# A transformer layer in one Trainium2 program: x's norm in the last four QKV blocks later and behind the evictions, x of two blocks loaded behind a quad of weights

## The chip, the cores and the metric

The program runs on one NeuronCore of one Trainium2 chip. The metric is the device time of one execution in microseconds, lower is better. The kernel before takes 2337.14 us, the median of three runs that lie between 2336.86 and 2337.38. The profile is of one further execution.

## What is computed

One pre-norm transformer layer in float32 on x of shape (2, 2048, 1024): attention with one head of 256, and a feed-forward part with a gate.

```python
def layer(x):
    x = x + attn(layernorm(x))
    return x + ffn(layernorm(x))

def attn(x):                      # D = 256
    q, k, v = split(x @ Wqkv + bqkv, 3)
    return softmax(q @ k.T / 16) @ v @ Wo + bo

def ffn(x):
    s = sum(top_k(x @ gate_w, 2))
    h = relu(x @ up_w) ** 2
    return layernorm(h @ down_w + s * (x @ fc1_w @ expert_w) @ fc2_w) * gamma + beta
```

The change touches only the first part of the program, where the first layernorm and `x @ Wqkv` are computed (QKV).

## The kernel before

**Stages.** The program runs through a short start, QKV (to some 327 us in the trace), attention, and the feed-forward part, which is most of the time. Every product is made of three matmuls: each operand is kept as a high part (rounded to fp32r, made on ScalarE by a copy) and a low part (what the rounding left, subtracted on VectorE), and high*high, high*low and low*high are added in PSUM.

**One list of steps.** `timetable()` writes the order of the whole program as one list of named steps; each engine goes through the list and issues only its own part of each step. In QKV the list is laid out by numbers g = 0 to 95, twelve for each of eight blocks of 512 rows of x (u or t = 0 to 7). In block t, g = 12t to 12t+7 are the halves of the four q and k products (`pe_qk`, lines 958 to 960) and g = 12t+8 to 12t+11 the four v products (`pe_v`, lines 977 to 979). `at(g, ...)` puts a step behind the TensorE work of g; `front(g, ...)` puts it behind the TensorE work of g too, but ahead of all steps that `at` put there. Each engine executes its own queue strictly in this order, the DMAs that it issues included, so a step that waits holds up all that stands behind it on its engine.

**The way of x in blocks 4 to 7.** SP loads x of the block into RAW (`load_x`, line 2186, four DMAs of 512 KB), once block u-2's last turn has been made (`raw_done`). VectorE takes the moments (`x_stats`, line 1552, 16 instructions), GpSimd merges them with a round trip through DRAM (`x_merge`, lines 2065 to 2129) and writes NBX and RX. ScalarE normalizes RAW in place (`x_norm`, line 1211, four instructions for each of j = 0 to 3), VectorE turns it (`x_turn`, line 1558, one for each j), ScalarE and VectorE make the high and low parts (`x_parts`, lines 1172 and 1497, into XA0 or XA1, h and l); every `x_parts` waits for the last turn of its block, as its first line says. The first `pe_qk` of the block waits for the low part.

**The evictions.** `qk_out` (line 1224, ScalarE, tiles OUT and STG) empties one of two PSUM banks. Product i of a block goes into bank i % 2, so `pe_qk` of (t, i) waits for `qk_out` of (t, i-2).

**Quads.** Beside this the kernel forms seven combinations of the four quarters of each feed-forward weight block and writes them to DRAM in high and low parts. One such job (a quad) is: SP loads it (lines 2288 and 2296) into the tiles QR0a or QR1a, VectorE makes sums (`quad_sums`, lines 1671 to 1678), ScalarE the high parts (`quad_high`, 1322 or 1325 and 1172), ScalarE issues their store (1330), VectorE makes the low parts (1686 to 1697), ScalarE issues their store (1337 to 1339, or 1341). Jobs 0 to 9 (u0 to u9) and job 10 (d0) alternate between the two buffers q0 and q1, at g = 4 + 11m/2. The load of a job waits for the stores of the job before it in its buffer. Smaller jobs in the buffers qd and qe (QRd, QRe) follow from g = 68.

**K and V.** From g = 67 SP loads K and V back from DRAM into two small STG buffers (`kv_load`, line 2231), and ScalarE and VectorE split them into KH/KL and VH/VL. KH lies where buffer q0 was, so its first split waits for the store of d0; a load into an STG buffer waits for the split of what was there. At g = 84 and 85 the last V splits and the split of Q stand ahead of `qk_out` of (7, 0). `Q`, `K` and `V` are what attention's first product needs.

```python
    def run(n):
        for step in ahead.pop(n, []) + later.pop(n, []):
...
        def raw_done(u):
            return normed["turn", u, 3] if u > 3 else xt_mm[u, 3]
...
        def x_parts(u, a):
            on.wait_ge(*normed["turn", u, 3])
```

Of the kernel before, what the change touches and what calls it, by code (L numbers as in the profile page):

```python
# [138 lines left out]
def timetable():  # L139
# [6 lines left out]
    def at(n, *step):  # L146
        later.setdefault(n, []).append(step)

    def front(n, *step):
        ahead.setdefault(n, []).append(step)  # L150
# [123 lines left out]
            at(n, "xt_hi", u, a)  # L274
            front(n + 1, "xt_lo", u, a)
    for u in range(4, 8):
        load, moments, norm = {4: (22, 28, 40), 5: (30, 37, 49), 6: (45, 51, 62), 7: (55, 61, 73)}[u]
        for tt in range(4):
            front(load, "load_x", u, tt)
            at(moments + tt // 2, "x_stats", u, tt)  # L280
        at(moments + 1, "x_merge", u)
        for j in range(4):
            front(norm + j, "x_norm", u, j)
            at(norm + 1 + j, "x_turn", u, j)
            front(norm + 5 + j // 2, "x_parts", u, j)
    for q, n0, times in ((("d", 1, 0), 68, (70, 71, 72, 72, 72, 73)), (("d", 1, 1), 75, (77, 78, 79, 79, 79, 80)),
                         (("d", 2, 0), 82, (85, 86, 87, 87, 87, 88)), (("d", 2, 1), 84, (86, 87, 88, 88, 88, 89)),
                         (("d", 3, 0), 91, ("S1", "S2", "S3", "S3", "S3", "S4"))):
# [182 lines left out]
    for s in range(4):  # L471
        u, d = 140 * s, 140 * s + 70
# [115 lines left out]
def transformer_layer(nc, x, wqk, wv, bqk, bv, wo, woT, bo, boc, gate, upfc, dn, expT, fc2, gamma, beta, out):  # L588
# [183 lines left out]
    tail_st = landed("tail")  # L772

    steps = timetable()

    def x1_stored(t, tt):
# [1759 lines left out]
```

## Time and profile before

| | |
|---|---|
| median of three runs | 2337.14 us (2336.86 to 2337.38) |
| the profiled execution's own time | 2336.3 us |
| its span, first to last instruction | 2334.5 us |
| mean granted TensorE clock over the span | 0.995 |
| TensorE matmul busy | 2301.9 us, 99% |
| VectorE / ScalarE / GpSimd busy | 68% / 35% / 15% |
| DMA, mean over the span | 249 GB/s |
| first matmul of q and k in blocks 3 to 7, us | 145.8, 186.0, 228.0, 266.3, 303.5 |

The span is 1.8 us shorter than the profiled execution's time, and that is 0.8 us below the median. A busy share is an average over stages with different limits. The views below are read for the stretch to 345 us, in which all of the change lies. "L1211" is line 1211 of the kernel; ACTq and SPq are the queues of ScalarE and SyncE from which DMAs are issued.

### The profile page before, as it was taken

How to read it: one execution, taken by the hardware profiler on the slowest of the kernel's cores; microseconds unless marked ns; L12 is line 12 of the kernel's file. 1: busy time of each engine (PE TensorE's matmuls, PEld its weight loads, DVE VectorE, ACT ScalarE, POOL GpSimd, SP SyncE). 2: the span in 40 equal slices, each digit the busy share in tenths (PEclk: the TensorE clock that was granted, in tenths of full speed). 3: DMA queues.
4: the chain of work that ended last, by engine and by line, in shares of the span. 5: the costliest groups of instructions: out<-in, count | busy, mean ns of one | idle time of the engine just before them, and what ended most of it. 6: DMA issues, size and time to landing. Idle time of an engine off the chain costs nothing.

```text
span 2334.5 us, 27523 instructions
## 1 busy us (share of the span) xinstructions
PE 2301.9 (99%) x10760; PEld 1931.3 (83%) x10760; DVE 1584.0 (68%) x1788; ACT 825.3 (35%) x949; POOL 344.7 (15%) x694
## 2 busy tenths in 40 slices
PE   9998899999999999999999999999999999999998
PEld 7887788888888888888888888888888888888886
DVE  6867658887898965498773368875249876434548
ACT  4345645666655442421221231213132121223211
POOL 2134400000132300032200023310003221000000
PEclk9999999999999999999999999999999999999999
DMA  9899873542334699978996678898668899666875
GB/s 286 302 374 329 306 244 123 203 145 77 109 109 128 245 300 342 315 271 306 346 316 209 194 263 294 316 335 270 191 223 273 309 329 328 213 191 204 240 209 195
DMA packets 242322, 581.19 MB, mean 249 GB/s; under 512 B 27345, under 2 KB 91793, under 8 KB 241937
## 3 DMA queue, kind: packets, MB, share of 16 engines
q1 hardware_dynamic: 160272, 443.56, 58.5%
q10 hardware_dynamic: 81280, 135.55, 16.0%
q8 instruction: 85, 1.39, 0.2%
q0 software_dynamic: 640, 0.33, 0.1%
q14 instruction: 45, 0.36, 0.0%
HBM read 422.25 MB, written 152.90 MB: 246 GB/s over the span
## 4 chain that ended last, share of the span: by engine, by line
PE 82%; DVE 5%; DMA 5%; ACT 2%; SPq 2%; POOL 2%; issue 1%; ACTq 0%; DVEq 0%; POOLq 0%
PE psum L1146 11%; PE psum L1148 11%; PE psum L1147 11%; PE psum L1125 10%; PE psum L1127 10%; PE psum L1126 10%; PE psum L1028 2%; PE psum L1030 2%; PE psum L1029 2%; PE psum L998 2%; PE psum L1000 2%; PE psum L999 2%; PE psum L1088 1%; PE psum L1081 1%; PE psum L1082 1%
## 5 line engine op out<-in xcount | busy, mean ns | idle before, releaser
L1814 DVE TENSOR_TENSOR HB<-HB,psum 128x1024 f32<-128x1024 f32 x135 | 163.1, 1218 | 299.5 <-PE psum L1127 299.5
L2036 POOL TENSOR_SCALAR veA<-mvA 128x1 f32<-128x1 f32 x32 | 31.2, 977 | 1252.5 <-DVE mvA L1722 1252.5
L1381 ACT ACTIVATE HB<-HB 128x1024 f32<-128x1024 f32 x64 | 67.9, 1060 | 306.9 <-DVE HB L1814 306.9
L1125 PE MATMUL psum<-XS2h,WR 128*128 128x512 f32 x280 | 109.4, 391 | 0.5 <-DVE XS2l L1497 0.5
L1125 PE MATMUL psum<-XS0h,WR 128*128 128x512 f32 x280 | 109.3, 390 | 0.0
L1125 PE MATMUL psum<-XS1h,WR 128*128 128x512 f32 x280 | 109.2, 390 | 0.0
L1125 PE MATMUL psum<-XS3h,WR 128*128 128x512 f32 x280 | 109.2, 390 | 0.0
L1127 PE MATMUL psum<-XS0h,WR 128*128 128x512 f32 x280 | 109.1, 390 | 0.0
L1127 PE MATMUL psum<-XS1h,WR 128*128 128x512 f32 x280 | 109.1, 390 | 0.0
L1126 PE MATMUL psum<-XS1l,WR 128*128 128x512 f32 x280 | 109.1, 390 | 0.0
L1127 PE MATMUL psum<-XS2h,WR 128*128 128x512 f32 x280 | 109.1, 390 | 0.0
L1126 PE MATMUL psum<-XS2l,WR 128*128 128x512 f32 x280 | 109.1, 390 | 0.0
L1126 PE MATMUL psum<-XS0l,WR 128*128 128x512 f32 x280 | 109.1, 390 | 0.0
L1126 PE MATMUL psum<-XS3l,WR 128*128 128x512 f32 x280 | 109.1, 390 | 0.0
L1127 PE MATMUL psum<-XS3h,WR 128*128 128x512 f32 x280 | 109.1, 390 | 0.0
L1028 PE MATMUL psum<-PH,VH 128*128 128x512 f32 x256 | 99.9, 390 | 0.1
L1030 PE MATMUL psum<-PH,VL 128*128 128x512 f32 x256 | 99.8, 390 | 0.0
L1029 PE MATMUL psum<-PL,VH 128*128 128x512 f32 x256 | 99.7, 390 | 0.0
L1497 DVE TENSOR_TENSOR PL<-SA,PH 128x1024 fp32r<-128x1024 f32 x64 | 78.1, 1220 | 18.1 <-ACT PH L1172 18.1
L1262 ACT ACTIVATE SA<-psum 128x1024 f32<-128x1024 f32 x64 | 65.3, 1022 | 58.3 <-PE psum L1000 55.2
L1273 ACT ACTIVATE SA<-SA 128x1024 f32<-128x1024 f32 x64 | 67.7, 1058 | 41.4 <-DVE SA L1611 28.5
L1611 DVE TENSOR_TENSOR SA<-SA,MB 128x1024 f32<-128x1024 f32 x64 | 77.1, 1214 | 3.0 <-ACT MB L1268 3.0
(439 smaller groups left out, 6701.7 us busy)
## 6 DMA issues: line engine op xcount, KB each, us to landing
WR<-wu_s SPq DMA_DIRECT2D x280, 512.0 KB, 4.3
WR<-wd_s SPq DMA_DIRECT2D x280, 512.0 KB, 5.0
att_s<-ATT ACTq DMA_DIRECT2D x32, 516.0 KB, 3.4
RAW<-in_x_dram SPq DMA_DIRECT2D x32, 512.0 KB, 9.1
RES<-x1b_s SPq DMA_DIRECT2D x128, 128.0 KB, 6.1
out_dram<-ZR ACTq DMA_DIRECT2D x118, 128.0 KB, 5.9
xT_s<-XT SPq DMA_DIRECT2D x24, 512.0 KB, 7.6
HB<-xT_s SPq DMA_DIRECT2D x12, 1024.0 KB, 8.6
```

The source lines that it names most:

```text
L1028: e.matmul(o, VH[:, kt, ds], h[:, c, :], start=kt == 0, stop=False)
L1029: e.matmul(o, VH[:, kt, ds], low[:, c, :], start=False, stop=False)
L1030: m = e.matmul(o, VL[:, kt, ds], h[:, c, :], start=False, stop=kt == 15)
L1125: e.matmul(o, w[:, 0, ws], h[:, :, ws], start=kt == 0, stop=False)
L1126: e.matmul(o, w[:, 0, ws], low[:, :, ws], start=False, stop=False)
L1127: m = e.matmul(o, w[:, 1, ws], h[:, :, ws], start=False, stop=kt == 3)
L1146: e.matmul(o, h[:, kt % 2, ts], w[:, 0, :], start=kt == 0, stop=False)
L1147: e.matmul(o, h[:, kt % 2, ts], w[:, 1, :], start=False, stop=False)
L1148: m = e.matmul(o, low[:, kt % 2, ts], w[:, 0, :], start=False, stop=kt == 9)
L1497: e.tensor_tensor(l, src, f(h), op=ALU.subtract).then_inc(*lo.next(key))
L1611: e.tensor_tensor(P_at(i, k), P_at(i, k), mb, op=ALU.subtract).then_inc(*sub.next((i, k)))
L1814: e.tensor_tensor(to, a, src, op=ALU.add).then_inc(*vevac.next(key))
```

## The change

Only numbers and the kind of placement in `timetable()` change, for blocks 4 to 7:

- `load_x` of block 5 moves from g = 30 to 33, which is behind the load of quad u5 (g = 31) on SP's queue; that of block 7 from 55 to 57, where no other load stands in between.
- `x_stats` and `x_merge` move from 37 to 40 in block 5 and from 61 to 62 in block 7.
- `x_norm` was placed ahead (`front`) of the eviction of its g, one j at each of four g; it is now behind it (`at`), two j at each of two g. It starts at 42, 54, 65 and 74 in place of 40, 49, 62 and 73.
- `x_turn` and `x_parts` follow in pairs of j, at one and at three or four g after the norm's start.

```diff
@@ -274,15 +274,15 @@
             at(n, "xt_hi", u, a)
             front(n + 1, "xt_lo", u, a)
     for u in range(4, 8):
-        load, moments, norm = {4: (22, 28, 40), 5: (30, 37, 49), 6: (45, 51, 62), 7: (55, 61, 73)}[u]
+        load, moments, norm = {4: (22, 28, 42), 5: (33, 40, 54), 6: (45, 51, 65), 7: (57, 62, 74)}[u]
         for tt in range(4):
             front(load, "load_x", u, tt)
             at(moments + tt // 2, "x_stats", u, tt)
         at(moments + 1, "x_merge", u)
         for j in range(4):
-            front(norm + j, "x_norm", u, j)
-            at(norm + 1 + j, "x_turn", u, j)
-            front(norm + 5 + j // 2, "x_parts", u, j)
+            at(norm + j // 2, "x_norm", u, j)
+            at(norm + 1 + j // 2, "x_turn", u, j)
+            front(norm + 3 + j // 2, "x_parts", u, j)
```

No instruction is added or removed. TensorE's and GpSimd's orders stay the same. On SyncE's queue one pair changes places, in block 2 (RAW_104 is x of the even, RAW_105 of the odd blocks; here x of block 5 and quad u5):

```order
@@ -29,6 +29,6 @@
 L2186 DMA RAW_104<-in_x_dram 32x16x256 x4
 L2288 DMA QR0a<-in_upfc_dram 128x4x512
+L2288 DMA QR1a<-in_upfc_dram 128x4x512
 L2186 DMA RAW_105<-in_x_dram 32x16x256 x4
-L2288 DMA QR1a<-in_upfc_dram 128x4x512
 L2288 DMA QR0a<-in_upfc_dram 128x4x512
 L2288 DMA QR1a<-in_upfc_dram 128x4x512
```

Quad u5 is now asked for before x of block 5, and not after it.

ScalarE's queue in block 5, from the high parts of quad d0 (L1325, L1172) to the issue of the store of its low parts (L1341); L1211 is the norm of block 6, L1224 an eviction, XA0h the high parts of block 6. Before:

```order
L1325 ACTIVATE QH0a<-QR0a 128x2048
L1172 ACTIVATE QH0a<-QR0a 128x1536
L1211 ACTIVATE RAW_104<-RAW_104,NBX,RX 128x256 x4
L1224 ACTIVATE OUT<-psum,bqs 128x512
L1330 DMA wd_s<-QH0a 128x7x512
L1229 DMA qk_s<-OUT 128x512
L1172 ACTIVATE XA0h<-XA0t 128x1024 x2
L1224 ACTIVATE OUT<-psum,bqs 128x512
L1172 ACTIVATE XA0h<-XA0t 128x1024 x2
L1229 DMA qk_s<-OUT 128x512
L1341 DMA wd_s<-QR0a 128x7x512
```

Changed:

```order
L1325 ACTIVATE QH0a<-QR0a 128x2048
L1172 ACTIVATE QH0a<-QR0a 128x1536
L1224 ACTIVATE OUT<-psum,bqs 128x512
L1211 ACTIVATE RAW_104<-RAW_104,NBX,RX 128x256 x8
L1330 DMA wd_s<-QH0a 128x7x512
L1229 DMA qk_s<-OUT 128x512
L1211 ACTIVATE RAW_104<-RAW_104,NBX,RX 128x256 x8
L1224 ACTIVATE OUT<-psum,bqs 128x512
L1172 ACTIVATE XA0h<-XA0t 128x1024 x2
L1229 DMA qk_s<-OUT 128x512
L1341 DMA wd_s<-QR0a 128x7x512
```

Of the 16 norm instructions of block 6, 12 stood ahead of the quad's high parts and 4 behind; now all 16 stand behind, and ahead of the store L1341.

ScalarE's queue in block 6, among the splits of K (KH); L1211 is the norm of block 7, L1341 the store of a small quad. Before:

```order
L1172 ACTIVATE KH<-STG 128x2x256
L1330 DMA wd_s<-QHd 128x7x256
L1211 ACTIVATE RAW_105<-RAW_105,NBX,RX 128x256 x4
L1224 ACTIVATE OUT<-psum,bqs 128x512
L1172 ACTIVATE KH<-STG 128x2x256
L1341 DMA wd_s<-QRd 128x7x256
L1211 ACTIVATE RAW_105<-RAW_105,NBX,RX 128x256 x4
L1229 DMA qk_s<-OUT 128x512
L1172 ACTIVATE KH<-STG 128x2x256
L1211 ACTIVATE RAW_105<-RAW_105,NBX,RX 128x256 x4
L1224 ACTIVATE OUT<-psum,bqs 128x512
L1172 ACTIVATE KH<-STG 128x2x256
```

Changed:

```order
L1172 ACTIVATE KH<-STG 128x2x256
L1330 DMA wd_s<-QHd 128x7x256
L1224 ACTIVATE OUT<-psum,bqs 128x512
L1172 ACTIVATE KH<-STG 128x2x256
L1341 DMA wd_s<-QRd 128x7x256
L1229 DMA qk_s<-OUT 128x512
L1211 ACTIVATE RAW_105<-RAW_105,NBX,RX 128x256 x8
L1172 ACTIVATE KH<-STG 128x2x256
L1224 ACTIVATE OUT<-psum,bqs 128x512
L1211 ACTIVATE RAW_105<-RAW_105,NBX,RX 128x256 x8
L1172 ACTIVATE KH<-STG 128x2x256
```

The first eviction no longer has norm ahead of it; the later K splits have runs of eight ahead of them where they had four.

## Rows read from the trace of the kernel before

**Rows 1.** The page: the chain that ended last, by engine.

```profile
PE 82%; DVE 5%; DMA 5%; ACT 2%; SPq 2%; POOL 2%; issue 1%; ACTq 0%; DVEq 0%; POOLq 0%
```

**Rows 2.** TensorE in order of time: start, us, what [idle before <-releaser].

```profile
160.76 0.79 PE L958 MATMUL psum<-XA1h,WQH 128*128 128x512 f32 x1 [3.92 <-ACT STG L1224]
203.66 0.79 PE L958 MATMUL psum<-XA0h,WQH 128*128 128x512 f32 x1 [6.60 <-ACT OUT L1224]
247.49 0.50 PE L958 MATMUL psum<-XA1h,WQH 128*128 128x512 f32 x1 [2.97 <-ACT OUT L1224]
280.29 0.51 PE L958 MATMUL psum<-XA0h,WQH 128*128 128x512 f32 x1 [2.98 <-ACT OUT L1224]
316.13 0.50 PE L958 MATMUL psum<-XA1h,WQH 128*128 128x512 f32 x1 [1.57 <-ACT OUT L1224]
```

**Rows 3.** Busy by stretch: PE, PEld, DVE, ACT, POOL; granted clock, DMA share, GB/s.

```profile
90.00:174.00 84.00, 79.39 (x451) 69.43 (x450) 61.87 (x103) 30.25 (x42) 24.23 (x57) 0.96 1.02 368
174.00:180.00 6.00, 6.00 (x50) 5.92 (x49) 4.30 (x6) 6.00 (x11) 2.20 (x4) 1.00 0.76 253
180.00:210.00 30.00, 23.40 (x119) 19.95 (x119) 21.94 (x30) 16.89 (x27) 17.06 (x32) 0.89 1.06 368
210.00:222.00 12.00, 12.00 (x77) 10.88 (x76) 8.63 (x16) 7.04 (x10) 4.02 (x7) 1.00 0.79 266
...
252.00:258.00 6.00, 6.00 (x41) 5.53 (x40) 4.93 (x4) 5.03 (x9) 2.19 (x4) 1.00 0.73 265
```

**Rows 4.** The chain that ended last, in order of time: start, us, what.

```profile
126.03 16.05 DMA wu_s<-QR1a
142.15 11.16 DMA QR1a<-in_upfc_dram
```

**Rows 5.** ScalarE in order of time: d0's store, first K and next to last V split.

```profile
259.91 0.63 ACTq L1341 DMA_DIRECT2D wd_s<-QR0a  x1
...
270.43 0.63 ACT L1172 ACTIVATE KH<-STG 128x512 fp32r<-128x512 f32 x1 [9.03 <-DMA wd_s<-QR0a]
...
314.36 0.63 ACT L1172 ACTIVATE VH<-STG 128x512 fp32r<-128x512 f32 x1 [3.13 <-DMA STG<-v_s]
```

**Rows 6.** DMA issues, the store L1339 at 167 us: KB, us to landing.

```profile
wu_s<-QR1a ACTq DMA_DIRECT2D x1, 1024.0 KB, 8.5
```

**Rows 7.** VectorE in order of time: block 4's last turn, sums of u8 and d0.

```profile
180.36 1.23 DVE L1558 STREAM_TRANSPOSE XA0t<-RAW 128x1024 f32<-128x1024 f32 x1
...
213.09 0.67 DVE L1671 TENSOR_TENSOR QR0a<-QR0a 128x512 f32<-128x512 f32 x1
...
247.46 0.69 DVE L1671 TENSOR_TENSOR QR0a<-QR0a 128x512 f32<-128x512 f32 x1 [0.77 <-DMA QR0a<-in_dn_dram]
```

**Rows 8.** ScalarE in order of time: high parts of quads, norm, x's part, issue.

```profile
176.01 1.91 ACT L1172 ACTIVATE QH0a<-QR0a 128x2048 fp32r<-128x2048 f32 x1
...
200.96 2.07 ACT L1211 ACTIVATE RAW<-RAW,NBX,RX 128x256 f32<-128x256 f32 x4 [5.75 <-POOL NBX L2123]
...
219.11 1.04 ACT L1172 ACTIVATE XA1h<-XA1t 128x1024 fp32r<-128x1024 f32 x1
...
229.82 0.44 ACTq L1337 DMA_DIRECT2D wu_s<-QE0a  x1
...
251.93 1.47 ACT L1172 ACTIVATE QH0a<-QR0a 128x1536 fp32r<-128x1536 f32 x1
```

**Rows 9.** SyncE's queue in order of time: loads of u8 and of block 7's x.

```profile
199.67 0.39 SPq L2288 DMA_DIRECT2D QR0a<-in_upfc_dram  x1
...
216.88 2.31 SPq L2186 DMA_DIRECT2D RAW<-in_x_dram  x4
```

**Rows 10.** DMA issues: load of u8, high and low store of d0, us to landing.

```profile
QR0a<-in_upfc_dram SPq DMA_DIRECT2D x1, 1024.0 KB, 8.2
...
wd_s<-QH0a ACTq DMA_DIRECT2D x1, 1792.0 KB, 6.9
...
wd_s<-QR0a ACTq DMA_DIRECT2D x1, 1792.0 KB, 10.4
```

## The prediction

> **What bounds the kernel now.** The page comes first: matmuls are busy for 99% of the span (the table), and the chain that ended last is 82% PE [rows 1]. So only the rest can be won, and TensorE's own timeline says where it is: in QKV it stands idle six times in front of L958, each time for an eviction (L1224), in blocks 3, 4, 5, 6 and 7: 3.92 + 6.60 + 2.97 + 2.98 + 1.57 us [rows 2], with a further 0.27 in block 6, 18.3 us in all. After the two longest the first matmul takes 0.79 us, and the granted clock is 0.96 and 0.89 in the stretches that hold them [rows 3]: 84 x 0.04 + 30 x 0.11 = 6.7 us of clock, less what falls into the idle time itself. 18.3 + 6.7 = 25.0 us is thus about the ceiling, and the norm of block 5 is the clearest case: ScalarE sat 5.75 us in it for GpSimd's NBX, with the eviction right behind it [rows 8].
>
> The third view asks which wait ends last, and it speaks against the ceiling. The chain of waits in order of time leaves TensorE at 126 us for a store of 16.05 us and a load of 11.16 us, and stays with the quads and x [rows 4]. ScalarE's timeline shows its end: the store of d0, issued at 259.91, lets the first K split start at 270.43; from there 16 splits follow one another, the next to last at 314.36, still waiting for its load [rows 5]. The eviction of (7, 0) stands behind that one, and TensorE goes on at 316.13 [rows 2]. **A gain before 316 us counts only as far as d0's store and the 44 us of K and V behind it move forward.** The loads of the small quads stand behind the V loads on SP's queue, so what follows moves with them too.
>
> And the DMA engines are full: a share of 1.02 and 1.06 in the long stretches, with three gaps [rows 3]. The unused share to 258 us is 6 x 0.24 + 12 x 0.21 + 6 x 0.27 = 5.6 us. The change moves no byte away.
>
> **The change part by part.** All shifts are against the rows' times.
>
> *x of block 5 behind quad u5 (SP).* The store that frees q1 took 16.05 us with x's four loads beside it [rows 4]; a later one of the same size took 8.5 [rows 6]. So this store ends 0 to 7.5 us sooner. I take 2: only some 0.8 of x's 2.1 MB had moved by then, at 368 GB/s [rows 3]. The quad's load no longer stands behind x either, so its sums (now at 142.15 + 11.16 = 153.3 [rows 4]) come some 6 us sooner, the high parts about 2.3 sooner (ScalarE is still busy issuing), and block 3's stall shrinks from 3.9 to about 1.6. The Trainium skill ("DMA: Bandwidth & Descriptors", Queues, rings and completion order) says that each DMA engine takes turns between the queues by packets; by that rule x's bytes are only dealt out later, out of the same share, and the store that frees q0 for u6 would not come sooner. The trace can't show that before the change is run; it agrees that the share is used up.
>
> *Block 4's start.* u6 in q0 is loaded when the store before it has landed; all bytes ahead of it are the same, so its sums and high parts stay where they are, within 1 us: the last high part ends at 176.01 + 1.91 = 177.9 [rows 8]. Before, 12 of 16 norm instructions were done by then, and the last turn started at 180.36 [rows 7]. Now 8 are done: an eviction (0.6) and 8 norms stand behind the high parts. Four norms take 2.07 [rows 8], so eight 4.1: last turn at about 182.1, +1.7. Turn, high and low part (1.2 + 1.0 + 1.2), with the quad's low part (2.3) in between, bring the first low part to about 186.7. Block 4 then starts some 0.7 later than before (186.0, the table), and TensorE, which came 4 to 7 us sooner, stands idle at the block's start instead of inside block 3. The gain of block 3 is spent.
>
> *Inside block 4.* The eviction of (4, 0) is not behind the norm any more: 6.60 and its clock go. u6's store, now behind the later turns, goes out 1.5 later, so u8's load is issued at 201.2 rather than 199.67 [rows 9] and lands 8.2 later [rows 10], at 209.4. Its sums waited for turns and moments until 213.09 [rows 7]; these now stand elsewhere, so the sums and high parts come about 4 sooner. But then 0.6 + 16 norms (8.2) follow: before, XA1h started at 219.11 [rows 8] right behind the high parts; now the last turn is at about 225. Block 5 starts at 227.3 (225 and a high and a low part), not 228.0: -0.7.
>
> *Inside block 5.* 2.97 and its clock go. u8's low store needs only the first pair of XA1h now, 227.5 rather than 229.82 [rows 8]: -2.3. But x of block 7 waits for block 5's last turn: issued at 225 rather than 216.88 [rows 9], so its 2.1 MB fall beside that store. 2.1 MB at 368 GB/s [rows 3] are 5.7 us, half of it ahead of the store: about +2.5. The two cancel: d0's sums stay at 247.46 [rows 7]; bounds -2.3 and +3.
>
> *Behind d0's high parts (251.93 + 1.47 = 253.4 [rows 8]).* Here the order of the queue decides. Before, 4 norms stood behind them; now an eviction and 16 do: 12 x 0.52 = 6.2 us more and 0.6 for the eviction up to the last turn, less 1.4 since one high part and one eviction fewer lie between that turn and the store: **L1341 goes out at 265.3, not 259.91, +5.4.** Block 6 starts at 265.7, not 266.3.
>
> *The landing.* The store took 10.4 us with loads of a small quad and of K beside it; the equal high store 6.9 [rows 10]. So it lands at 265.3 + 6.9 to 10.4 = 272.2 to 275.7. I take 272.5, near the lower end, since most of what lay beside it is over by then: **+2.2** against 270.3. If nothing of this is so (d0 2.3 sooner), it is about 0.
>
> *Block 6 and on.* The eviction of (6, 0) no longer waits for 4 norms (-2.1), which the late K splits take back. The eight-norm runs hold up the fifth and seventh K split by up to 3.7, and with them the V loads; ScalarE's whole work there is the same, so I take 0, bound +3.7. The cover is that the V splits in block 6 wait for ScalarE's other work too.
>
> Sum: +2.2 on the end of the chain, and with it on the end. Against the profiled run's 2336.3 us that is 2338.5; it lies 0.8 below the median, so the median forecast is 2337.1 + 2.2 = **2339.3 us**.
>
> **The rivals.**
>
> *The stalls go and little comes in their place (faster).* For it: 18.3 us of idle are real [rows 2], most evictions there wait behind norm or a quad's high parts, and quad u8's 4 us could go on to d0. Against: DMA's unused share is 5.6 us. If all of it is used and the last stall (1.57) goes, the time is 2337.1 - 7.2 = 2329.9. This decides once d0's store lands before 266 us. Chance 0.20.
>
> *All stalls go.* 18.3 us, and up to 6.7 of clock: 2337.1 - 18.3 = 2318.8, at best 2312.1. The rows against it are the chain's [rows 4, 5]: K and V alone are 44 us of loads in a row. Chance 0.05. The Trainium skill ("Perfetto Trace Analysis", Optimization Strategies) says to keep TensorE going by dealing with what it waits for; by that rule the evictions are the whole matter, and this would be the outcome.
>
> *d0's store and K (slower).* If the landing moves by the full 5.4, as it does when what lies beside the store moves with it, and the eight-norm runs cost V their full 3.7, the K and V chain ends 9.1 later: 2346.2. For it: L1341 behind 16 norms is certain from the order. Against: it had 3.5 us of neighbours to lose [rows 10]. It decides once the first K split starts after 275.0. Chance 0.22.
>
> *Nothing moves.* GpSimd's NBX, not the queue, holds the norm, and DMA sets the rest: 2337.1. Chance 0.03; block 5's norm alone waited for GpSimd that long.
>
> **How the numbers follow.** About 0.2% (4.7 us) is what a measurement of this kernel can surely tell from no change. My forecast has 0.50, with its own range of 2334.0 (d0 2.3 sooner and its landing or V 3 us better than taken) to 2341.8 (the threshold); with "nothing moves" that makes 0.53 within 0.2%. Faster: 0.20 + 0.05 = 0.25. Slower: 0.22. For 8 in 10 the range takes in the first rival with some clock on top (2327) and the slower one (2347).
>
> **What would show it.** Right: TensorE's stalls in front of L958 in blocks 4 and 5 gone, and idle time of 3 to 6 us at the starts of blocks 4, 5 and 6 behind XA0l or XA1l (L1497) in their place; d0's L1341 issued at 263 to 267 us; the first K split at 271 to 275; the eviction of (7, 0) at 316 to 320. Wrong: block 4 starting before 182 us (then u6 was not held by DMA), or the first K split before 267 (faster), or after 276 (slower).

## The result, and the profile after

The changed kernel takes 2348.73 us, the median of four runs that lie between 2347.62 and 2349.69. The kernel before took 2337.00 (2335.18 to 2337.38) beside it. The ratio is 1.0052, with a 95% interval of 1.0034 to 1.0069: slower by some 12 us, not level. The profiled execution took 2347.6 us with a span of 2345.8, 11.4 more than before.

Start where the prediction started. The page of the changed kernel, the chain of waits by engine:

```profile
PE 83%; DMA 8%; DVE 4%; ACT 2%; SPq 2%; issue 1%; POOL 0%; ACTq 0%; DVEq 0%; POOLq 0%
```

Against [rows 1] DMA has 8% for 5%; where, the page doesn't say, so the place has to be found in time. TensorE in order of time, changed kernel (start, us, what, idle before and its releaser), the answer to [rows 2]:

```profile
159.62 0.50 PE L958 MATMUL psum<-XA1h,WQH 128*128 128x512 f32 x1 [3.83 <-ACT STG L1224]
...
187.71 0.47 PE L958 MATMUL psum<-XA0h,WQH 128*128 128x512 f32 x1 [3.67 <-DVE XA0l L1497]
...
230.41 0.76 PE L958 MATMUL psum<-XA1h,WQH 128*128 128x512 f32 x1 [7.46 <-DVE XA1l L1497]
...
270.38 0.77 PE L958 MATMUL psum<-XA0h,WQH 128*128 128x512 f32 x1 [3.68 <-DVE XA0l L1497]
...
285.22 0.50 PE L958 MATMUL psum<-XA0h,WQH 128*128 128x512 f32 x1 [2.19 <-ACT OUT L1224]
...
293.66 0.50 PE L958 MATMUL psum<-XA0h,WQH 128*128 128x512 f32 x1 [2.71 <-ACT OUT L1224]
...
328.18 0.79 PE L958 MATMUL psum<-XA1h,WQH 128*128 128x512 f32 x1 [4.68 <-ACT OUT L1224]
```

The stalls inside blocks 4 and 5 are gone, and blocks 4, 5 and 6 now start with one behind x's low parts. The seven add up to 28.2 us, where there were 18.3. The last row is the important one: TensorE goes on behind the eviction of (7, 0) at 328.18, 12.05 us later than before, and what follows is as long as before within 1 us (2017.6 us to the end of the span, 2018.3 before).

What made that eviction late is in the chain of waits in order of time, changed kernel, from u8's load (start, us, what):

```profile
201.93 9.80 DMA QR0a<-in_upfc_dram
...
216.08 1.80 ACT QH0a L1172
217.89 0.46 ACT RAW L1211 x2
...
218.77 3.06 ACT RAW L1211 x6
...
229.51 12.91 DMA wu_s<-QR0a
...
242.92 9.21 DMA QR0a<-in_dn_dram
...
256.62 1.47 ACT QH0a L1172
258.09 0.40 ACT OUT L1224
258.57 2.12 ACT RAW L1211 x5
261.03 1.58 ACT RAW L1211 x3
262.64 1.25 DVE XA0t L1558
263.88 1.64 DVE QR0a L1697
265.52 2.31 DVE XA0t L1558 x2
267.86 0.40 ACT XA0h L1172
268.30 8.81 DMA wd_s<-QR0a
```

The norm (L1211) stands on this chain between the quads' high parts and their stores. The same stretch of the kernel before:

```profile
230.80 7.92 DMA wu_s<-QR0a
...
239.22 8.22 DMA QR0a<-in_dn_dram
...
251.93 1.48 ACT QH0a L1172
253.44 2.29 DVE QR0a L1692
255.73 1.16 DVE XA0t L1558
...
258.93 0.57 ACT OUT L1224
...
259.91 10.41 DMA wd_s<-QR0a
```

Here four norms stand between d0's high parts and its store in ScalarE's queue, and none of them is on the chain. The two chains give the account:

| term | before, us | after, us | difference |
|---|---|---|---|
| u8's load issued | 199.67 | 201.93 | +2.3 |
| load, parts and turns, to the low store (L1339) | 31.13 | 27.58 | -3.6 |
| the low store, 1 MB | 7.92 | 12.91 | +5.0 |
| d0's load | 8.22 | 9.21 | +1.0 |
| end of d0's high parts | 253.40 | 258.09 | +4.7 in all |
| from there to the issue of L1341 | 6.51 | 10.21 | +3.7 |
| landing of L1341 | 10.41 | 8.81 | -1.6 |
| first K split | 270.43 | 277.22 | +6.8 in all |
| first K split to next to last V split | 43.93 | 49.18 | +5.25 |

The 5.25 are the third view. ScalarE in the K and V stretch, changed kernel:

```profile
288.47 4.04 ACT L1211 ACTIVATE RAW<-RAW,NBX,RX 128x256 f32<-128x256 f32 x8 [2.15 <-issue]
292.42 0.61 ACT L1172 ACTIVATE KH<-STG 128x512 fp32r<-128x512 f32 x1
...
294.00 3.54 ACT L1211 ACTIVATE RAW<-RAW,NBX,RX 128x256 f32<-128x256 f32 x7
297.44 1.14 ACT L1172 ACTIVATE KH<-STG 128x512 fp32r<-128x512 f32 x2
301.10 2.01 ACT L1172 ACTIVATE XA1h<-XA1t 128x1024 fp32r<-128x1024 f32 x2 [2.52 <-DVE XA1t L1558]
...
305.48 0.62 ACT L1172 ACTIVATE VH<-STG 128x512 fp32r<-128x512 f32 x1
```

The sixth K split stands behind eight norm instructions, the seventh behind eight more (20.2 us after the first split; before it was 286.88 - 270.43 = 16.5). Then ScalarE sits 2.52 us for block 7's turns, and the first V split, behind the high parts, comes 28.3 us after the first K split and not 23.4. Each late split also frees its STG buffer late, so the next load goes out late.

One more view tells what became of the DMA's unused share. One stretch of the changed kernel (columns as in [rows 3]):

```profile
226.00:230.00 4.00, 0.00 (x0) 0.00 (x0) 2.88 (x3) 2.33 (x3) 3.19 (x13) 0.50 0.24 68
```

and the same stretch of the kernel before:

```profile
226.00:230.00 4.00, 4.00 (x28) 3.68 (x27) 4.00 (x5) 0.00 (x0) 1.06 (x2) 1.00 1.06 395
```

While TensorE waits for block 5's norm and turns, at a granted clock of 0.50, the lower of its two levels (1.2 GHz), the DMA engines are three quarters idle too (share 0.24). Neither of the two large transfers that come next can go out then: x's buffer is free only with block 5's last turn (x of block 7 is loaded from 227.93 on, not 216.88), and the store of u8's low parts stands on ScalarE behind the high parts that wait for the turns. Both then fall on the same microseconds.

### The profile page after: what moved, and what is told of

The parts are those of the page before. It is cut to its first block, busy times and chain, and to the rows that moved or that the text cites. A ratio compares the mean times of both kernels' runs of the same rounds, so it can differ in the third digit from the quotient of the medians.

```text
span 2345.8 us, 27523 instructions
## 1 busy us (share of the span) xinstructions
PE 2305.2 (98%) x10760; PEld 1935.4 (83%) x10760; DVE 1584.8 (68%) x1788; ACT 826.0 (35%) x949; POOL 352.9 (15%) x694
## 4 chain that ended last, share of the span: by engine, by line
PE 83%; DMA 8%; DVE 4%; ACT 2%; SPq 2%; issue 1%; POOL 0%; ACTq 0%; DVEq 0%; POOLq 0%
PE psum L1146 11%; PE psum L1148 11%; PE psum L1147 11%; PE psum L1125 10%; PE psum L1127 10%; PE psum L1126 10%; PE psum L1028 2%; PE psum L1030 2%; PE psum L1029 2%; PE psum L998 2%; PE psum L1000 2%; PE psum L999 2%; DMA wu_s<-QR0a 2%; DMA QR0a<-in_upfc_dram 1%; PE psum L1088 1%; PE psum L1081 1%
## 5 line engine op out<-in xcount | busy, mean ns | idle before, releaser
L2036 POOL TENSOR_SCALAR veZ<-mvZ 128x4 f32<-128x4 f32 x7 | 7.7, 1102 | 482.8 <-DVE mvZ L1965 482.8
```

## The experiments

The theory: the end is set by d0's store and the K and V chain behind it, and each block's late norm delays one link. The rivals: that the stalls at the block starts are the loss, or x's loads by themselves. All kernels below were timed beside the kernel before. The table holds the marks of the chain in each one's profile, in us:

| kernel | u8's low store, issued to landed | d0's high parts end | L1341, issued to landed | next to last V split | span | median, ratio [95%] |
|---|---|---|---|---|---|---|
| before | 230.8 to 238.7 | 253.4 | 259.9 to 270.3 | 314.4 | 2334.5 | |
| changed | 229.5 to 242.4 | 258.1 | 268.3 to 277.1 | 326.4 | 2345.8 | 2348.73, 1.0052 [1.0034, 1.0069] |
| undo4 | 228.0 to 241.4 | 256.8 | 267.0 to 275.8 | 324.1 | 2346.4 | 2347.50, 1.0046 [1.0032, 1.0061] |
| undo5 | 232.1 to 239.7 | 256.3 | 266.5 to 275.4 | 324.7 | 2345.1 | 2347.64, 1.0047 [1.0032, 1.0062] |
| undo6 | 231.2 to 243.3 | 259.0 | 265.5 to 275.3 | 324.1 | 2344.7 | 2346.64, 1.0044 [1.0029, 1.0059] |
| undo7 | 229.4 to 242.7 | 258.2 | 268.4 to 277.2 | 321.4 | 2340.8 | 2344.02, 1.0034 [1.0022, 1.0047] |
| only5 | 227.4 to 240.9 | 256.5 | 263.0 to 272.6 | 316.8 | 2337.1 | 2339.68, 1.0017 [1.0008, 1.0026] |
| only6 | 230.5 to 238.4 | 254.8 | 265.0 to 273.8 | 318.0 | 2340.6 | 2338.82, 1.0014 [1.0005, 1.0023] |
| only7 | 230.4 to 238.5 | 254.2 | 260.7 to 270.8 | 319.9 | 2341.3 | 2341.74, 1.0025 [1.0015, 1.0034] |
| runs4 | 229.0 to 242.3 | 257.9 | 268.1 to 276.8 | 320.9 | 2341.8 | 2344.84, 1.0038 [1.0024, 1.0053] |
| x7late | 228.0 to 233.7 | 252.0 | 268.8 to 277.9 | 327.1 | 2348.1 | 2352.33, 1.0068 [1.0053, 1.0083] |
| evfirst | 229.6 to 237.8 | 254.4 | 261.3 to 270.2 | 314.3 | 2336.0 | 2337.76, 1.0005 [0.9996, 1.0014] |
| storeahead | 228.7 to 241.9 | 257.5 | 261.5 to 270.0 | 318.3 | 2337.6 | 2341.34, 1.0023 [1.0013, 1.0032] |
| lowahead | 229.9 to 237.8 | 252.6 | 256.6 to 267.6 | 312.1 | 2332.1 | 2334.42, 0.9992 [0.9983, 1.0000] |

The difference of the last two marks is 2019.3 to 2022.7 us in all fourteen: whatever is done, the end follows the next to last V split. The profiled executions lie up to 3.7 us from their medians (only6's above, x7late's 2.4 below), so costs are taken from medians and the marks are used for the terms. The kernel before beside the changed kernel had a median of 2337.00, beside the four undo kernels 2336.07: a difference between medians of two groups can be 0.9 us off, and both are given where it matters.

All but lowahead are written with the loop below and a table `plan` of places (undo4 to undo7 with an `if` on u to the same effect). undo4 to undo7, runs4 and x7late differ from the changed kernel in one entry of that table, only5 to only7 from the kernel before; the diffs below show that entry alone: load, moments, placement, then the places of norm, turns and parts for j = 0 to 3. The line numbers of undo4 to undo7 are five higher than those of the kernel before, of the others one higher, of lowahead the same. The loop:

```diff
+        load, moments, place, norm, turn, part = plan[u]
...
+            (front if place == "front" else at)(norm[j], "x_norm", u, j)
+            at(turn[j], "x_turn", u, j)
+            front(part[j], "x_parts", u, j)
```

### undo7, only7, runs4: block 7 and the K and V stretch

undo7 is the changed kernel with block 7 as before; only7 is the kernel before with block 7 as changed; runs4 is the changed kernel with block 7's norm still behind the evictions, but in four runs of four instructions, the first one step earlier and the last one step later, and with turns and parts spread as before.

```diff
undo7
-    7: (57, 62, 'at', (74, 74, 75, 75), (75, 75, 76, 76), (77, 77, 78, 78))
+    7: (55, 61, 'front', (73, 74, 75, 76), (74, 75, 76, 77), (78, 78, 79, 79))
only7
-    7: (55, 61, 'front', (73, 74, 75, 76), (74, 75, 76, 77), (78, 78, 79, 79))
+    7: (57, 62, 'at', (74, 74, 75, 75), (75, 75, 76, 76), (77, 77, 78, 78))
runs4
-    7: (57, 62, 'at', (74, 74, 75, 75), (75, 75, 76, 76), (77, 77, 78, 78))
+    7: (57, 62, 'at', (73, 74, 75, 76), (74, 75, 76, 77), (78, 78, 79, 79))
```

> Block 7 alone as before (load 55, moments 61, norm ahead of the evictions at 73 to 76), blocks 4 to 6 as changed. Chain theory (the end is set by d0's store and the K and V loads behind it): d0's store still lands near 277, but the K and V part is as long as before, since ScalarE has runs of four norms among the K splits again: the eviction of (7, 0) 5.3 us sooner than in the changed kernel, 2343.4. Rival (TensorE's own idle time at block starts and inside blocks adds up): block 6 gives back 2.19 + 2.71 and 1.7 of clock and takes 3.25: 2345.4.

> Blocks 4 to 6 as before, block 7 alone as changed. Chain theory: d0's store lands as before (K splits from 270.4), and the stretch from the first K split to the eviction that block 7 waits for is 5.2 us longer, 50.9 in place of 45.7: 2336.1 + 5.2 = 2341.3. Rival (idle time inside the blocks adds up): block 6 stands 4.9 and 1.7 of clock in place of 3.25: 2339.4.

> The changed kernel, but block 7's norm in four runs of four (73 to 76), each behind the eviction of its place, turns one by one. If the runs of eight are what lengthens K and V, the stretch is 45 to 46.5 us again and the time 2343.5. If it is that norm now stands behind the eviction and starts later, the stretch stays near 51 and the time at 2348.

Measured from the first K split to the next to last V split: 44.1 us in undo7 and 43.9 in runs4, which have the rest of the change, and 49.0 in only7, which has nothing else of it; before 43.9, changed 49.2. So the 5.25 us come from block 7's norm in two runs of eight, with its turns and parts in pairs, and from nothing ahead of it; that the norm stands behind the evictions is not what costs them. The length of the runs and the pairing of the turns were not taken apart. ScalarE in runs4 shows four norm instructions between splits, and no split that waits for more; its first V split comes 23.6 us after the first K split, as before (23.4) and not 28.3:

```profile
288.16 2.08 ACT L1212 ACTIVATE RAW<-RAW,NBX,RX 128x256 f32<-128x256 f32 x4 [0.80 <-issue]
290.14 0.61 ACT L1173 ACTIVATE KH<-STG 128x512 fp32r<-128x512 f32 x1
```

By medians block 7 costs 2341.74 - 2336.39 (the kernel before beside it) = 5.4 us alone, as the theory had it (2341.3) and not the rival (2339.4). undo7's 2344.02 alone would not settle it: it lies 0.6 above the theory's 2343.4 and 1.4 below the rival's 2345.4. That runs4 stands slightly above undo7 by its ratio is within their intervals.

### undo6, only6: what stands ahead of d0's store

```diff
undo6
-    6: (45, 51, 'at', (65, 65, 66, 66), (66, 66, 67, 67), (68, 68, 69, 69))
+    6: (45, 51, 'front', (62, 63, 64, 65), (63, 64, 65, 66), (67, 67, 68, 68))
only6
-    6: (45, 51, 'front', (62, 63, 64, 65), (63, 64, 65, 66), (67, 67, 68, 68))
+    6: (45, 51, 'at', (65, 65, 66, 66), (66, 66, 67, 67), (68, 68, 69, 69))
```

> Block 6 alone as before (norm ahead of the evictions at 62 to 65). Chain theory: 12 of 16 norms of block 6 are done before d0's high parts again, so d0's low store goes out 3.7 us sooner and all behind it moves with it: 2345.0, down to 2343.3 if the full 5.4 of the forecast come back. Rival (idle time adds up): the 3.68 at block 6's start and its clock go, the 2.97 inside block 5 and its clock come back: 2348.0, no difference.

> The kernel before with block 6 alone changed (load, moments, norm, turn and parts of block 6 as in the changed kernel). Chain theory: d0's high parts stay at 253.4 +-1 us, the issue of the store of d0's low parts (L1341) moves from 259.9 to 263.6 behind the sixteen norm instructions (+3.7, the difference between 6.5 and 10.2 us seen in the profiles of before and of the changed kernel), the store lands in 8.8 to 10.4 us, K and V take their 45.7 us: the first K split at 272.6 to 274.1, median 2338.5 to 2340.1 beside 2336.4 for the kernel before. Rival (the stall inside block 6 is worth something, the store is not): 2333.5 to 2336.4.

ScalarE in only6:

```profile
253.35 1.47 ACT L1173 ACTIVATE QH0a<-QR0a 128x1536 fp32r<-128x1536 f32 x1
...
255.78 7.49 ACT L1212 ACTIVATE RAW<-RAW,NBX,RX 128x256 f32<-128x256 f32 x15
263.18 0.67 ACT L1225 ACTIVATE OUT<-psum,bqs 128x512 f32<-128x512 f32 x1
...
265.03 0.46 ACTq L1342 DMA_DIRECT2D wd_s<-QR0a  x1
```

From the end of d0's high parts to the store it takes 10.2 us in only6 and the changed kernel, 6.5 in undo6 and before. The 3.7 us of the order are thus block 6's alone. The store lands in 8.8 us in the first two, in 9.8 in undo6 and 10.4 before. Cost alone, by medians: 2338.82 - 2336.23 = 2.6 us. undo6's 2346.64 lies above what the theory expected of it and below the rival. Its chain starts 0.9 later (259.0) and its landing gives 1.0 back, so in the full change block 6 is worth less than its 3.7: 2.1 us between the two medians, 1.2 with each set against the kernel before beside it, 2.3 at the V split.

### undo5, only5, x7late: x of block 7 beside u8's store

```diff
undo5
-    5: (33, 40, 'at', (54, 54, 55, 55), (55, 55, 56, 56), (57, 57, 58, 58))
+    5: (30, 37, 'front', (49, 50, 51, 52), (50, 51, 52, 53), (54, 54, 55, 55))
only5
-    5: (30, 37, 'front', (49, 50, 51, 52), (50, 51, 52, 53), (54, 54, 55, 55))
+    5: (33, 40, 'at', (54, 54, 55, 55), (55, 55, 56, 56), (57, 57, 58, 58))
x7late
-    7: (57, 62, 'at', (74, 74, 75, 75), (75, 75, 76, 76), (77, 77, 78, 78))
+    7: (60, 65, 'at', (74, 74, 75, 75), (75, 75, 76, 76), (77, 77, 78, 78))
```

> Block 5 alone as before (load 30 ahead of quad u5, moments 37, norm at 49 to 52). Chain theory: block 5's last turn is early again, x of block 7 is loaded from about 217 and does not lie beside u8's low store, so d0's sums come 4.7 sooner (247.5) and the end with them: 2344.0. Rival (idle time adds up): the 7.46 at block 5's start and 5 of clock go, the 6.60 inside block 4 and 1.9 of clock come back: 2344.8, so this run alone doesn't tell them apart by time; the time of d0's sums does (the rival has no opinion on it).

> The kernel before with block 5 alone changed, so x of block 5 behind quad u5 and x of block 7 asked for only when block 5's late turns are made. Chain theory: u8's load goes out near 199.7 as before; the low store of u8 goes out 2 us sooner (228.5), but takes 12 to 13 us and not 7.9 with x of block 7 beside it, and d0's load 9 to 10 and not 8.2: d0's high parts end at 255.5 to 257 (before 253.4), L1341 at 262 to 263.5, landing 8.8 to 10.4 later, K and V 45.7: median 2338 to 2339.5. Rival (x beside the store costs nothing, the lateness came from u8's late load alone): 2334 to 2336.4.

> The changed kernel, but x of block 7 is loaded behind d0 on SP's queue (g = 60) and its moments follow at 65. If x beside u8's low store is what made that store take 12.9 us, it takes 8 again, d0 is loaded 5 sooner and the end comes 3 to 5 sooner: 2344 to 2346. Rival (the store shares with whatever else is queued, and GpSimd's NBX of block 7 comes too late): no gain, 2348.7 or more.

The store L1339 of u8 takes 7.6 us in undo5 and 7.9 before, where x of block 7 was loaded earlier; 12.9 and 13.6 in the changed kernel and in only5, where it is loaded beside it; and 5.7 in x7late, where it is loaded behind d0. That is the term which the prediction had at +2.5. only5 came in where the theory put it (2339.68, just above its 2339.5; 3.45 above 2336.23), and its rival (2334 to 2336.4) is out.

undo5 missed both forecasts. The store is 5.3 us shorter than in the changed kernel, but goes out 2.6 later, since u8's low parts stand behind x's on VectorE again, as before, and d0's load takes 10.1 us and not 9.2: 1.8 us are left at d0's high parts. The median is 1.1 us below the changed kernel's, and 0.2 with each set against the kernel before beside it; neither is told from none.

x7late missed by 6 us and more, on the slower side, and is the most telling miss. Its rival's time, 2348.7 or more, is the one that came. d0's load landed at 239.3, 13 us sooner than in the changed kernel, and d0's store went out at 268.8, no sooner. VectorE in x7late, and the start of block 7's norm on ScalarE:

```profile
254.56 2.71 DVE L1553 BATCH_NORM_STATS2 STX<-RAW 128x6 f32<-128x256 f32 x8 [11.19 <-DMA RAW<-in_x_dram]
257.19 2.27 DVE L1693 TENSOR_TENSOR QR0a<-QR0a,QH0a 128x2048 fp32r<-128x2048 f32 x1
...
261.67 2.67 DVE L1553 BATCH_NORM_STATS2 STX<-RAW 128x6 f32<-128x256 f32 x8
264.26 1.74 DVE L1698 TENSOR_TENSOR QR0a<-QR0a,QH0a 128x1536 fp32r<-128x1536 f32 x1
...
289.97 4.04 ACT L1212 ACTIVATE RAW<-RAW,NBX,RX 128x256 f32<-128x256 f32 x8 [2.84 <-POOL NBX L2124]
```

Block 7's moments stand ahead of d0's low parts on VectorE, and waited 11.19 us for x, which now came late. A load pushed out of one link's way held up the next link through another engine's queue. The same late moments made GpSimd's NBX late, as the rival had said, and the chain that ended last runs through it and no longer through d0's store; the rival's other half, that the store would share with whatever else is queued, is out (5.7 us). At the V split all this comes to 0.7 us over the changed kernel, while the spans are 2.3 apart and the medians 3.6; what makes the rest is not shown.

### undo4, evfirst: the stalls of TensorE

```diff
undo4
-    4: (22, 28, 'at', (42, 42, 43, 43), (43, 43, 44, 44), (45, 45, 46, 46))
+    4: (22, 28, 'front', (40, 41, 42, 43), (41, 42, 43, 44), (45, 45, 46, 46))
evfirst
-    'front'
+    'at'
```

evfirst is the kernel before with `x_norm` behind the eviction of its g in all four blocks, and nothing else.

> Block 4 alone as before (norm ahead of the evictions at 40 to 43). Chain theory: u6's store goes out some 2 us sooner, of which DMA takes most: 2347.7, 0 to 2 less than the changed kernel. Rival (idle time adds up): the 3.67 at block 4's start and 1.7 of clock go and nothing comes back, as the norm of block 4 was not what block 3 waited for: 2343.3.

> The kernel before with each norm piece behind the eviction of its own g and nothing else moved: loads, moments, numbers, turns and parts as before. Chain theory: the stalls behind the evictions shrink or go (6.60 in block 4, 2.98 in block 6), but nothing on the way to d0's store or K and V moves by more than an eviction: 2335 to 2337, no difference. Rival (idle time adds up): 8 to 12 us less, 2325 to 2328.

undo4 has 0.8 us of wait at block 4's start and not 3.7, and block 5's start has 9.4 and not 7.5. Its time is 2347.50, 1.2 below the changed kernel (0.3 with each set against the kernel before beside it) with intervals that overlap widely: the rival that counts stalls (2343.3) is out. evfirst took 2337.76 beside 2336.39, 0.8 above what the theory had and 10 us above its rival. In it TensorE waited 10.5 + 5.7 us inside the blocks and 1.6 at block 4's start, 17.8 in all, and before 18.3: the wait inside block 4 shrank (6.60 to 2.80), and another grew inside block 6 (2.98 to 5.71).

```profile
204.94 0.79 PE L959 MATMUL psum<-XA0h,WQH 128*128 128x512 f32 x1 [2.80 <-ACT STG L1225]
...
278.22 0.80 PE L959 MATMUL psum<-XA0h,WQH 128*128 128x512 f32 x1 [5.71 <-ACT OUT L1225]
```

With the chain's marks at their old places, what TensorE saves in one block it waits in a later one. TensorE went on behind the eviction of (7, 0) at 316.1 in both.

### storeahead, lowahead: the store itself moved

storeahead is runs4 with d0's low parts and their store ahead of the second half of block 6's norm; lowahead is the kernel before with the second low part ahead of block 6's last turn, and the store ahead of block 6's high parts.

```diff
storeahead
+            ... ((4, 5, 6, 6, 6, 6) if m == 10 else (3, 4, 5, 5, 6, 8) if g0 < 37 else (4, 5, 6, 6, 7, 9))])
lowahead
-            ... ((3, 4, 5, 5, 6, 8) if g0 < 37 else (4, 5, 6, 6, 7, 9))])
+            ... ((4, 5, 6, 6, 6, 7) if m == 10 else (3, 4, 5, 5, 6, 8) if g0 < 37 else (4, 5, 6, 6, 7, 9))])
```

> The changed kernel with block 7's norm in runs of four as in the kernel of that experiment (2344.8), and quad d0's low parts and their store ahead of the second eight of block 6's norm. Chain theory: L1341 goes out at 262 to 263 and not at 268.1, lands 8.8 to 10.4 later; the first K split at 271 to 273, 4 to 6 us sooner than 276.95; K and V 45.7: median 2339 to 2341. Rival (what is late is x and the blocks, not this store): 2344 to 2345.

> The kernel before, and only quad d0's second low part (L1697) goes ahead of block 6's last turn on VectorE and its store (L1341) ahead of block 6's high parts and one eviction on ScalarE. Chain theory: low parts end at 257.4, L1341 goes out there and not at 259.9 (-2.5), the first K split at 268 to 269; block 6 starts some 1.7 later, which is not on the chain as long as TensorE's 1.6 us of stall in block 7 is left to cover it: median 2334 to 2336 beside 2336.4. Rival (TensorE and the chain are now equally late, or the store merely takes longer): within 1 us of 2336.4. Rival (block 6's late start goes to the end): 2337.5 to 2338.5.

storeahead: the store went out 4.0 us behind d0's high parts and landed at 270.0, where the kernel before had it; the ratio fell from runs4's 1.0038 to 1.0023. By medians it gains 3.5 (2344.84 and 2341.34). The landing came 6.8 us sooner than in runs4, the first K split only 4.2 (272.8), since on ScalarE it stands behind block 6's high parts, and these wait for the last turn:

```profile
268.46 1.06 ACT L1173 ACTIVATE XA0h<-XA0t 128x1024 fp32r<-128x1024 f32 x1 [0.74 <-DVE XA0t L1559]
...
272.76 0.63 ACT L1173 ACTIVATE KH<-STG 128x512 fp32r<-128x512 f32 x1 [0.39 <-issue]
```

Block 6's late norm thus has a second hold on the chain, as soon as the store is out of the way.

lowahead, in its chain of waits:

```profile
252.62 2.29 DVE QR0a L1692
254.92 1.68 DVE QR0a L1697
256.62 10.95 DMA wd_s<-QR0a
```

Between high parts and store there are 4.0 us and not 6.5. It took 2334.42 us beside 2336.23: 1.8 less, a ratio of 0.9992 with an interval that reaches 1.0000. It is the fastest version found, and lies where the theory had it (2334 to 2336); that it is a gain at all is likely and not certain. Some 0.9 us of its 2.3 at the next to last V split were there already at u8's store (229.9 for 230.8), ahead of the edit. The store took 10.95 us for 10.41, so 0.5 of the 2.5 went to a slower landing.

### The parts added up

Alone, blocks 5, 6 and 7 cost 3.45 + 2.59 + 5.35 = 11.4 us by medians, each to some 2 us either way by its interval, and the whole change 11.7. Block 4 alone was not run. Undoing it in the full change gives at most 1.2 back, and undoing block 5 at most 1.1, where block 5 alone costs 3.45; how these two share their part is not settled.

## Why the prediction was wrong

The forecast was 2339.3 (2327 to 2347), the result 2348.73. The mechanism that bounds the kernel was read rightly; it was called the slower rival with a chance of 0.22 and 2346.2 us, and it decided ("once the first K split starts after 275.0": 277.22). It too was short, with 9.1 us at the V split where 12.0 came: the landing moved by 6.8 and not 5.4, and K and V by 5.25 and not 3.7. The forecast went wrong in three terms of its sum.

- *"The two cancel"* (u8's low store against x of block 7): d0's sums were to stay at 247.46, bounds -2.3 and +3. They came at 252.15, **+4.7**, out of the bounds. The store went out only 1.3 sooner and not 2.3, x beside it cost 5.0 and not 2.5, and d0's load took 1.0 more, for which there was no term. The step priced x by its bytes (2.1 MB, half ahead of the store), while an earlier row already had a store of this size at 16.05 us with x beside it and 8.5 without [rows 4, 6]. That row was no clean price either: in the changed kernel the same store (124.73, the one that frees q1) still took 13.8 us with x of block 5 asked for only after it.
- *"Block 6 and on"*: taken as 0, bound +3.7; **+5.25**. The argument was that ScalarE's whole work is the same. But in a chain of loads each split frees the buffer of the next load, so it counts when the splits come, not how much work there is. The 3.7 was right for the seventh K split (+3.8); the other split with eight norms ahead of it is the sixth, not the fifth. What stood behind it was left out: block 7's turns and high parts ahead of the first V split (+4.9).
- *"The landing"*: the store was to take 7.2 us, since what lay beside it would be over. It took 8.81 (**+1.6**).

Against these stands one term that was too dear: from the end of d0's high parts to L1341 the prediction had 6.5 + 5.4 = 11.9 us; it took 10.2. Together: 4.7 + 3.7 - 1.6 + 5.25 = 12.0 at the V split, where the sum had 0 + 5.4 - 3.2 + 0 = 2.2.

By its other steps:

- *x of block 5 behind quad u5.* The store that frees q1 ended 3.5 us sooner (138.6 for 142.1) of which 1.3 lay in its earlier issue: 2 was right. u5's sums came 6.9 us sooner, 6 was said. But block 3's stall stayed at 3.83, where 1.6 was forecast. ScalarE was issuing DMAs until 154.9, and the high parts came only 1.1 sooner. The parenthesis "ScalarE is still busy issuing" was in the text and its price was not.
- The Trainium skill ("DMA: Bandwidth & Descriptors", Queues, rings and completion order) has each DMA engine take turns between the queues by packets. By that rule x's bytes would only be dealt out later, and the store that frees q0 not come sooner. The trace agrees: that store landed at 162.9, before at 162.0.
- *Block 4's start*: 186.7 forecast, 187.71 measured. *Inside block 4*: u8's load at 201.2 forecast, 201.93 measured; its landing 8.2 taken, 9.8 measured. *Block 5's start*: 227.3 forecast, 230.41 measured; *block 6's*: 265.7 and 270.38.
- The marks named beforehand: stalls gone inside blocks 4 and 5 and back at the starts behind XA0l or XA1l, as said, though 7.46 us in block 5 and not 3 to 6; L1341 at 268.3, above 263 to 267; the first K split above 276, which was named as the sign of slower; the eviction of (7, 0) at 327.5, not 316 to 320.
- The rival "all stalls go" (2318.8) is excluded. The Trainium skill ("Perfetto Trace Analysis", Optimization Strategies) says to keep TensorE going by optimizing the engines that block the critical path. The evictions were what TensorE waited for, and not what set that path: evfirst took them out from behind the norm, and the time stayed (1.0005 [0.9996, 1.0014]).

The chances were the second fault. Two of the three terms passed their upper bound, and the third lay in the middle of its bounds; all three had been taken at or near the low end, each with a reason of its own. The rival that was built from two of the upper bounds should have been the forecast, and a range up to 2347 still would not have held 2348.73.

## What to carry to other kernels

Where a chain of loads and stores sets the end, list each engine instruction that stands ahead of a link of it in its queue, and price a moved one by the delay of that link and of all that follow in the chain, not by the engine's total work. Keep long runs of other work (here eight norms, 4 us) out of a stretch in which an engine also frees the buffers of loads. An idle gap of TensorE that a later gap takes over is worth nothing; the mark to move is the issue of the store that something waits for.

## What was not expected of the hardware

How much a neighbour costs one transfer. The 1 MB store L1339 of u8 took 7.6 to 8.3 us where x of block 7 was loaded ahead of it, 12.2 to 13.6 where the four loads of 512 KB lay beside it, and 5.7 where they came behind it.

The instruction that issues a DMA can itself hold the engine's queue for microseconds. ScalarE in block 3 of the changed kernel:

```profile
147.76 4.12 ACTq L1339 DMA_DIRECT2D wu_s<-QR0a  x1
151.92 2.94 ACTq L1234 DMA_DIRECT2D v_s<-OUT  x1
154.90 0.63 ACT L1322 ACTIVATE QH1a<-QR1a 128x512 fp32r<-128x512 f32 x1 [13.17 <-issue]
...
163.67 0.57 ACTq L1339 DMA_DIRECT2D wu_s<-QR1a  x1
```

The same line takes 4.12 us at 147.76 and 0.57 at 163.67. In x7late such an issue (L1230, 4.37 us from 244.30) held ScalarE until d0's high parts: their sums came 11.4 us sooner than in the changed kernel, they themselves only 6.1. The profile does not show what the long ones wait for, and no run tested it.
